# A language adapter with layer norm on one core: the order of the beginning is changed, and where the first products get their weights

## The chip, the cores and the metric

The kernel runs on one core of one Trainium2 chip. The metric is the device time of one execution in microseconds (us), the median of the runs shown.

## What is computed

For 128 samples of 128 rows and 512 columns (float32), each with the number of one of ten languages:

```python
w1 = W1[language_ids]            # 10 tables of 512 x 128
w2 = W2[language_ids]            # 10 tables of 128 x 512
h = relu(einsum('bsh,bha->bsa', x, w1) + b1[language_ids])
y = x + einsum('bsa,bah->bsh', h, w2) + b2[language_ids]
out = x + (y - mean(y)) * rsqrt(var(y) + 1e-5) * gamma[language_ids] + beta[language_ids]
```

## The kernel before

The samples are worked in 64 pairs. Ten pairs of x fit into `x_io` (SLOTS is 20), and the results are written over x in the same slots and stored from there.

**What a pair costs on each engine.** TensorE turns the two samples (`turn_x`, L488: 8 transposes of 128x128 into `ps_T`), ScalarE copies them to `x_T` (L401), TensorE makes the first product (`first_products`, L497 for b1, L504 for 8 products in float32, recorded as 16 matmuls), ScalarE takes relu and rounds it (`high_h`, L415), VectorE takes the rest of the rounding (`low_h`, L631). The second product (`second_product`, L525) is three matmuls of 512 columns for each sample, high by high, high by low and low by high, added into a bank of `ps_y` that VectorE (L644) or ScalarE (L431, every fourth sample; b2 is then added by a matmul, L519) has seeded with x + b2. ScalarE squares (L421), VectorE scales by gamma, inverts the deviation and finishes (L663, L668, L676). GpSimd adds beta to x (L358) and forms the mean (L353).

**TensorE's loop.** Iteration p does the second product of pair p - 2, turns pair p + 1, and does the first product of pair p (L552 to L573).

**The tables.** gamma, beta and b2 of all ten languages are needed on all 128 partitions. b2 is loaded there by a broadcast of 2.6 MB (L282). gamma and beta are loaded as 30 rows, cut into three bf16 parts (gamma on VectorE, L590 to L596; beta, and then b2 with its mean taken off by ScalarE, on GpSimd, L336 to L341), and spread over the partitions by 20 matmuls against a one-hot table (L544, "spread"). Six PSUM banks take the result in turn, and ScalarE (L457) or VectorE (L684) copies it out. For the first four samples b2 is put into the bank by such a matmul as well (`put_b2`, L511), before VectorE adds x (`seed_early`, L654). W2 is loaded into the x slots of pairs 5 to 9 in five chunks of two languages, its row means are taken off, and it is split into `w2_high` (ScalarE, L407) and `w2_low` (VectorE, L625). W1 is loaded into `w1_all` in five chunks (L287) in runs of 512 bytes. The first six pairs (STAGE_HBM) take their two W1 tables from HBM, also in runs of 512 bytes; later ones take one by a DMA from `w1_all` and the other by a copy of ScalarE (L440).

**What sets the order.** Every engine's order is written out by hand, with semaphores. The queue of SyncE (SP) issues nearly all transfers, in this order (L252 to L305): ids, gamma rows, x of pair 0, W1 of pair 0, W2 chunks 0 and 1, x 1, W1 of pair 1, W2 chunks 2 to 4, x 2, W1 of pair 2, b2, x 3, W1 of pair 3, all five chunks of W1, then, after waits for gamma and beta, x 4, W1 of pairs 4 and 5, and x 5 to 9, each behind the split of a chunk of W2. From then on, for each pair p: W1 of pair p + 6, the store of pair p, the load of pair p + 9. TensorE's beginning is: turn pair 0, 20 spread matmuls, turn pair 1, first product 0, turn pair 2, first product 1, and then the loop proper, whose first second product waits for all of W2:

```python
if p >= FIRST:
    n = p - FIRST
    if n == 0:
        pe.wait_ge(w2_low_ready, L)
    for b in range(2):
        second_product(2 * n + b, langs[n][b])
pe.wait_ge(x_T_ready, p + 1)
```

ScalarE's beginning is: copy x 0, ten copies of gamma, high parts of W2 chunks 0 and 1, six copies of beta, copy x 1, and then W2 chunks 2 to 4 between copies of x and relu steps (L459 to L472).

Of the kernel before, what the change touches and what calls it, by code (L numbers as in the profile page):

```python
# [5 lines left out]
F32 = mybir.dt.float32  # L6
F32R = mybir.dt.float32r
# [6 lines left out]
SLOTS = 20  # L14
Y_BANKS = 4
# [3 lines left out]
STAGE_HBM = 6  # L19
FIRST = 2  # L20
EARLY = 2
W2_AHEAD = 2


def build(nc, x, ids, w1, b1, w2, b2, gamma, beta, out):
# [8 lines left out]
    ROWS_PAIR = X_FIRST - 1  # L34
# [3 lines left out]
    w1_rows = w1.rearrange("l (c p) a -> p l c a", c=C)  # L38
    out_pairs = out.rearrange("(n b) s h -> s n b h", b=2)
# [3 lines left out]
    SPREAD_BANKS = Y_BANKS + 2  # L43
    by_act = [n for n in range(2 * L) if n not in (L, L + 2, L + 4, L + 6)]
    by_dve = [n for n in range(2 * L) if n not in by_act]
    assert FIRST + 1 <= H_PAIRS

    with ExitStack() as ctx:
# [22 lines left out]
        cut = sb("cut", [128, 2, H], BF16)  # L71
        parts = sb("parts", [128, 3 * H], BF16)
        b2_rows = sb("b2_rows", [3 * L, H], F32)
        b2_cut = sb("b2_cut", [3 * L, 2, H], BF16)
        b1_rows = sb("b1_rows", [3 * L, A], F32)
# [8 lines left out]
        pick = sb("pick", [128, L, 128], BF16)  # L84
# [11 lines left out]
        squares = cut  # L96
# [35 lines left out]
        b2_centred = sem("b2_centred")  # L132
        seeded_act = sem("seeded_act")
# [14 lines left out]
        b2_in_bank = sem("b2_in_bank")  # L148
# [33 lines left out]

        def scalar_seeds(t):
            return len([u for u in range(t + 1) if by_scalar(u)])
# [4 lines left out]
        def scalar_copies(q):  # L189

            return q >= STAGE_HBM

        def w1_copies(q):
            return len([r for r in range(q + 1) if scalar_copies(r)])

        def w1_stagings(q):

            return sum(16 if scalar_copies(r) else 32 for r in range(q % STAGE_PAIRS, q + 1, STAGE_PAIRS))
# [35 lines left out]
        spread_banks = ps_y + ps_h  # L234
        assert len(spread_banks) == SPREAD_BANKS

        def spread_bank(n):
            return spread_banks[n % SPREAD_BANKS][:, :]

# [8 lines left out]
        def _(sp):  # L248
            def load_x(p):
# [3 lines left out]
            sp.dma_start(x_io[0:3 * L, 2 * ROWS_PAIR, :],  # L253
                         gamma.unsqueeze(0).broadcast_to([3, L, H])).then_inc(s_gamma_rows, 16)
            load_x(0)
# [4 lines left out]
            def stage_w1(q):  # L260

                langs = langs_of(sp, q)
                if q >= STAGE_PAIRS:
                    sp.wait_ge(h_summed, q - STAGE_PAIRS + 1)
                if q >= STAGE_HBM:
                    sp.wait_ge(s_w1, 16 * W_CHUNKS)
                table = w1_rows if q < STAGE_HBM else w1_all
                for b in range(1 if scalar_copies(q) else 2):
                    sp.dma_start(w1_stage[:, 2 * (q % STAGE_PAIRS) + b, :, :], table[:, bass.ds(langs[b], 1), :, :])\  # L269
                        .then_inc(w1_staged[q % STAGE_PAIRS], 16)  # L270

            sp.wait_ge(ids_ready, 1)
# [10 lines left out]
            load_x(3)  # L283
            stage_w1(3)
            for n in range(W_CHUNKS):
                langs = slice(n * LC, (n + 1) * LC)
                sp.dma_start(w1_all[:, langs, :, :], w1_rows[:, langs, :, :]).then_inc(s_w1, 16)  # L287
            sp.wait_ge(gamma_parts_ready, 1)
            sp.wait_ge(beta_parts_ready, 1)
            for p in range(4, X_FIRST):  # L290
                load_x(p)
            for q in range(STAGE_PAIRS, STAGE_AHEAD):
                stage_w1(q)
            for n in range(W_CHUNKS):
                sp.wait_ge(w2_low_ready, (n + 1) * LC)
                load_x(X_FIRST + n)

            for p in range(PAIRS - 1):
                if p + STAGE_AHEAD < PAIRS:
                    stage_w1(p + STAGE_AHEAD)  # L300
                sp.wait_ge(out_ready, 2 * p + 2)
                sp.dma_start(out_pairs[:, p, :, :], x_pair_slots(p)).then_inc(stored[p % X_PAIRS], 16)
                if p >= 1 and p - 1 + X_PAIRS < PAIRS:
                    sp.wait_ge(stored[(p - 1) % X_PAIRS], x_loads(p - 1))
                    load_x(p - 1 + X_PAIRS)  # L305
# [8 lines left out]
        def _(pool):  # L314
# [29 lines left out]
            pool.wait_ge(parts_zero, 3)  # L344
            pool.wait_ge(s_beta_rows, 16)
            cut_in_three(x_io[0:3 * L, 2 * ROWS_PAIR + 1, :], b2_cut[:, 0, :], parts[0:3 * L, H:2 * H], 0, beta_parts_ready)
            pool.wait_ge(b2_centred, 1)
            cut_in_three(b2_rows[:, :], b2_cut[:, 1, :], parts[0:3 * L, 2 * H:3 * H], 4, b2_parts_ready)
# [14 lines left out]
            pool.wait_ge(spread_dve, len(by_dve))  # L363
            for n in range(PAIRS):
# [12 lines left out]
        def _(act):  # L377
            act.wait_ge(set_ready, 4)
            nc.scalar.activation(table_load[:, :], eps[:, :], ACT.Sqrt, bias=eps[:, 0:1])
            act.dma_start(b1_rows[:, :],  # L380
                          b1.unsqueeze(0).broadcast_to([3, L, A])).then_inc(s_b1_rows, 16)
            act.dma_start(x_io[0:3 * L, 2 * ROWS_PAIR + 1, :],
                          beta.unsqueeze(0).broadcast_to([3, L, H])).then_inc(s_beta_rows, 16)
            act.dma_start(b2_rows[:, :],
                          b2.unsqueeze(0).broadcast_to([3, L, H])).then_inc(s_b2_rows, 16)
            act.wait_ge(pick_step, 3)
            nc.scalar.copy(pick[:, :, :], pick_row[:, :].unsqueeze(2).broadcast_to([128, L, 128])).then_inc(pick_ready, 1)

            act.wait_ge(s_b2_rows, 16)
            nc.scalar.activation(b2_cut[:, 1, :], b2_rows[:, :], ACT.Identity, accum_out=b2_sum[:, :])\  # L390
                .then_inc(b2_summed, 1)
            act.wait_ge(b2_summed, 1)
            nc.scalar.mul(b2_neg_mean[:, :], b2_sum[:, :], -1.0 / H).then_inc(b2_mean_ready, 1)
            act.wait_ge(b2_mean_ready, 1)
            nc.scalar.activation(b2_rows[:, :], b2_rows[:, :], ACT.Identity, bias=b2_neg_mean[:, :]).then_inc(b2_centred, 1)
# [47 lines left out]
            def step(p):  # L443
# [6 lines left out]
                q = p + STAGE_PAIRS - 1  # L450
                if q < PAIRS and scalar_copies(q):
                    copy_w1(q)
# [6 lines left out]
            copy_x(0)  # L459
# [4 lines left out]
            for n in by_act[L:]:  # L464
                copy_spread(n)
            copy_x(1)
            high_w2(2)
            high_h(0)
            high_w2(3)
            copy_x(2)  # L470
            high_h(1)
            high_w2(4)  # L472
# [10 lines left out]
        def _(pe):  # L483
            def turn_x(t):
                if t % 2 == 0:
                    pe.wait_ge(x_loaded[t // 2 % X_PAIRS], x_loads(t // 2))
                for c in range(C):
                    last = nc.tensor.transpose(ps_T[:, t % 2, c, :], x_io[:, t % SLOTS, c * 128:(c + 1) * 128],  # L488
                                               identity[:, :])
                last.then_inc(x_turned, 1)  # L490

            def first_products(p):
# [7 lines left out]
                if scalar_copies(p):  # L500
                    pe.wait_ge(w1_copied, w1_copies(p))
# [8 lines left out]
            def put_b2(t, lang):  # L510
                nc.tensor.matmul(ps_y[t % Y_BANKS][:, :], of_lang(pick, lang), parts[:, 2 * H:3 * H],  # L511
                                 start=True, stop=True).then_inc(b2_in_bank, 1)

            def second_product(t, lang):
# [3 lines left out]
                if by_scalar(t):  # L518
                    nc.tensor.matmul(bank, is_lang[:, t:t + 1].broadcast_to([128, S]), parts[:, 2 * H:3 * H],  # L519
# [9 lines left out]
            pe.wait_ge(identity_ready, 1)  # L529
            turn_x(0)  # L530
            turn_x(1)
            pe.wait_ge(pick_ready, 1)
            pe.wait_ge(parts_zero, 3)
            pe.wait_ge(gamma_parts_ready, 1)
            for n in range(2 * L):
                if n == L:
                    pe.wait_ge(beta_parts_ready, 1)
                gone = n - SPREAD_BANKS
                if gone in by_act:
                    pe.wait_ge(spread_act, by_act.index(gone) + 1)  # L540
                if gone in by_dve:
                    pe.wait_ge(spread_dve, by_dve.index(gone) + 1)
                table = parts[:, 0:H] if n < L else parts[:, H:2 * H]
                nc.tensor.matmul(spread_bank(n), pick[:, n % L, :], table, start=True, stop=True).then_inc(spread, 1)  # L544

            pe.wait_ge(ids_ready, 1)
            langs = {0: langs_of(pe, 0)}
            pe.wait_ge(b1_parts_ready, 1)
            pe.wait_ge(is_lang_ready, 1)
            pe.wait_ge(spread_act, len(by_act))  # L550
            pe.wait_ge(spread_dve, len(by_dve))
            for p in range(PAIRS):  # L552
# [183 lines left out]
```

## Time and profile before

| | us |
|---|---|
| median of 3 runs (316.99 to 318.69) | 318.01 |
| the profiled execution | 316.75 |
| its span | 315.0 |
| TensorE busy | 289.5 (92%) |
| VectorE busy | 289.8 (92%) |
| ScalarE busy | 263.0 (83%) |
| GpSimd busy | 186.2 (59%) |

The profile is of one execution, and its span is 1.75 us under that execution's time. Busy time of TensorE is a record of pipelined matmuls whose ends are modelled, so the interval between starts says more than their durations. The profile moved 94.03 MB, at 298 GB/s over the span.

### The profile page before, as it was taken

The page shows a single profiled execution, that of the slowest core. Times are in us where ns is not written, and L with a number is a line of the kernel's source. Part 1 is how long each engine was busy: PE and PEld are TensorE (multiplying, and loading weights), DVE is VectorE, ACT ScalarE, POOL GpSimd, SP SyncE. Part 2 cuts the span into 40 slices and gives each one's busy share as a digit, 9 for nine tenths or more (in the row PEclk, how much of TensorE's full clock was granted, in tenths as well). Part 3 has the DMA queues.
Part 4 walks back from the last instruction along what each step waited for, and adds up shares of the span by engine and source line. Part 5 has one row for each costly group of instructions (what it writes and reads, how often), then busy time and mean ns, then how long its engine had stood idle before and what let it go on. Part 6 is the DMA issues. An engine that isn't in the chain of part 4 may idle for free.

```text
span 315.0 us, 7506 instructions
## 1 busy us (share of the span) xinstructions
PE 289.5 (92%) x2008; PEld 253.8 (81%) x2039; DVE 289.8 (92%) x621; ACT 263.0 (83%) x601; POOL 186.2 (59%) x217
## 2 busy tenths in 40 slices
PE   1757959999999999999999999999999999999972
PEld 1237758889998888998888998888999888999861
DVE  5998856999999999999999999999999999999996
ACT  3977438889988889899989988999989988988872
POOL 2960742666655666565566665656656566665562
PEclk9968779999999999999999999999999999999998
DMA  5999999899999999899898989999898889885324
GB/s 155 332 389 372 293 331 390 276 340 352 358 347 328 321 313 302 302 318 318 292 315 313 299 309 310 318 302 311 290 319 311 315 304 311 286 291 202 116 110 177
DMA packets 56441, 94.03 MB, mean 298 GB/s; under 512 B 3387, under 2 KB 14711, under 8 KB 56273
## 3 DMA queue, kind: packets, MB, share of 16 engines
q1 hardware_dynamic: 56302, 93.41, 87.4%
q8 instruction: 18, 0.29, 0.4%
q14 instruction: 22, 0.18, 0.2%
q10 hardware_dynamic: 99, 0.14, 0.1%
HBM read 44.78 MB, written 33.55 MB: 249 GB/s over the span
## 4 chain that ended last, share of the span: by engine, by line
PE 79%; SPq 10%; issue 3%; DMA 3%; DVE 2%; DVEq 1%; ACT 0%
PE ps_h L504 33%; PE ps_y L525 28%; PE ps_T L488 16%; SPq L287 5%; DMA x_io<-in_x 2%; PE ps_h L497 2%; SPq L269 2%; SPq L257 1%; SPq L282 1%; DVE ps_y L663 1%; DVE ps_y L644 1%; SPq L172 1%; SPq L250 1%; DVEq L172 1%; DMA ids_raw<-in_itok_B 1%
## 5 line engine op out<-in xcount | busy, mean ns | idle before, releaser
L358 POOL TENSOR_TENSOR x_io<-x_io,beta_all 128x512 f32<-128x512 f32 x128 | 163.0, 1284 | 37.3 <-DVE ps_y L644 27.9
L504 PE MATMUL ps_h<-x_T,w_stage 128*128 128x128 f32 x1024 | 126.2, 277 | 0.0
L504 PEld LDWEIGHTS ps_h<-x_T,w_stage 128*128 128x128 f32 x1024 | 121.0, 194 | 0.8
L421 ACT ACTIVATE cut<-ps_y,row_sum 128x512 bf16<-128x512 f32 x128 | 87.9, 687 | 16.3 <-PE ps_y L525 11.4
L676 DVE SCALAR_TENSOR_TENSOR x_io<-ps_y,rstd,x_io 128x512 f32<-128x512 f32 x128 | 90.2, 747 | 2.6 <-DVE rstd L668 0.3
L663 DVE SCALAR_TENSOR_TENSOR ps_y<-ps_y,neg_mean,gamma_all 128x512 f32<-128x512 f32 x128 | 90.3, 750 | 1.7 <-ACT cut L421 1.7
L488 PE MATMUL ps_T<-identity,x_io 128*128 128x128 f32 x512 | 69.4, 280 | 11.2 <-DMA x_io<-in_x 10.1
L488 PEld LDWEIGHTS ps_T<-identity,x_io 128*128 128x128 f32 x512 | 62.2, 145 | 20.8 <-issue 12.6
L401 ACT COPY x_T<-ps_T 128x1024 f32<-128x1024 f32 x64 | 63.5, 992 | 6.7 <-PE ps_T L488 6.5
L525 PE MATMUL ps_y<-w_high,h_high 128*128 x128 | 62.3, 486 | 3.9 <-DVE w_low L625 2.2
L644 DVE SCALAR_TENSOR_TENSOR ps_y<-x_io,b_all 128x512 f32<-128x512 f32 x93 | 62.9, 704 | 0.0
L353 POOL TENSOR_TENSOR neg_mean<-row_sum,neg_over_h 128x2 f32<-128x2 f32 x64 | 12.9, 201 | 79.0 <-DVE ps_y L644 50.5
L525 PE MATMUL ps_y<-w_high,h_low 128*128 x128 | 51.2, 400 | 0.0
L525 PE MATMUL ps_y<-w_low,h_high 128*128 x128 | 50.6, 395 | 0.0
L440 ACT COPY w_stage<-w_all 128x512 f32 x58 | 36.0, 621 | 10.3 <-issue 8.7
L631 DVE SCALAR_TENSOR_TENSOR h_low<-ps_h,h_high 128x256 fp32r<-128x256 f32 x64 | 26.9, 420 | 4.3 <-ACT h_high L415 4.3
L525 PEld LDWEIGHTS ps_y<-w_high,h_high 128*128 128x128 f32 x128 | 24.9, 194 | 6.6 <-issue 4.9
L415 ACT ACTIVATE h_high<-ps_h 128x256 fp32r<-128x256 f32 x64 | 24.3, 380 | 5.8 <-PE ps_h L504 5.6
L525 PEld LDWEIGHTS ps_y<-w_high,h_low 128*128 128x128 f32 x128 | 24.3, 190 | 5.7
L525 PEld LDWEIGHTS ps_y<-w_low,h_high 128*128 128x128 f32 x128 | 24.7, 193 | 2.3
L421 ACT ACTIVATION_READ_ACCUMULATOR cut<-ps_y,row_sum 128x1 f32 x128 | 24.8, 194 | 0.0
L424 ACT ACTIVATE std<-sq_sum,eps 128x2 f32<-128x2 f32 x64 | 18.9, 295 | 2.1
(67 smaller groups left out, 150.9 us busy)
## 6 DMA issues: line engine op xcount, KB each, us to landing
x_io<-in_x SPq DMA_DIRECT2D x64, 512.0 KB, 5.1
out<-x_io SPq DMA_DIRECT2D x63, 512.0 KB, 3.9
w_stage<-w_all SPq DMA_DIRECT2D x58, 256.0 KB, 3.3
w_stage<-in_L_cond_W SPq DMA_DIRECT2D x12, 256.0 KB, 6.5
x_io<-in_L_cond_W SPq DMA_DIRECT2D x5, 512.0 KB, 7.8
b_all<-in_L_cond_b SPq DMA_DIRECT2D x1, 2560.0 KB, 14.3
w_all<-in_L_cond_W SPq DMA_DIRECT2D x5, 512.0 KB, 7.2
out<-x_io SPq DMA_DIRECT2D x2, 256.0 KB, 2.0
```

The source lines that it names most:

```text
L358: nc.gpsimd.tensor_tensor(x_slot(t), x_slot(t), of_lang(beta_all, lang), ALU.add).then_inc(x_beta_ready, 1)
L401: nc.scalar.copy(x_T[:, slots, :, :].rearrange("p b c s -> p (b c s)"), ps_T[:, :, :, :].rearrange("p b c s -> p (b c s)")).then_inc(x_T_r ...
L415: nc.scalar.activation(flat(h_high[:, p % H_PAIRS, :, :]), pair_of(ps_h[p % 2]), ACT.Relu)\
L421: nc.scalar.activation(squares[:, t % 2, :], ps_y[t % Y_BANKS][:, :], ACT.Square, scale=-float(H), bias=stat(row_sum, t), accum_out=stat(s ...
L440: nc.scalar.copy(w1_stage[:, 2 * (q % STAGE_PAIRS) + 1, :, :].rearrange("p c a -> p (c a)"), w1_all[:, bass.ds(lang, 1), :, :].rearrange(" ...
L488: last = nc.tensor.transpose(ps_T[:, t % 2, c, :], x_io[:, t % SLOTS, c * 128:(c + 1) * 128], identity[:, :])
L504: last = nc.tensor.matmul(bank[:, b * S:(b + 1) * S], w1_stage[:, 2 * (p % STAGE_PAIRS) + b, c, :], x_T[:, (2 * p + b) % 4, c, :], start=F ...
L525: last = nc.tensor.matmul(bank, h_part[:, h, b, :], of_lang(w2_part, lang), start=False, stop=False, skip_group_check=True)
L631: nc.vector.scalar_tensor_tensor(flat(h_low[:, p % H_PAIRS, :, :]), pair_of(ps_h[p % 2]), 0.0, flat(h_high[:, p % H_PAIRS, :, :]).bitcast( ...
L644: nc.vector.scalar_tensor_tensor(ps_y[t % Y_BANKS][:, :], x_slot(t), 1.0, of_lang(b2_all, langs[b]), ALU.mult, ALU.add, accum_out=stat(row ...
L663: nc.vector.scalar_tensor_tensor(bank, bank, stat(neg_mean, t), of_lang(gamma_all, langs[b]), ALU.add, ALU.mult).then_inc(scaled, 1)
L676: nc.vector.scalar_tensor_tensor(x_slot(t), ps_y[t % Y_BANKS][:, :], stat(rstd, t), x_slot(t), ALU.mult, ALU.add).then_inc(out_ready, 1)
```

## The change

- **Transfers.** All five chunks of W2 are issued ahead of x 0. Then come W1 and x of pairs 0 to 4 (W1 of 0 to 3), then b2, behind a wait for the cut parts of b1, b2, beta and gamma, then x 5, W1 of 4, x 6, W1 of 5. The chunks of `w1_all` move into the steady loop, one each in its first five turns. W1 of 12 pairs (before: 6) comes from HBM, both tables by DMA, in runs of 2 KB; for that, x of these pairs is turned with a step of four columns. `x_io` has 24 slots (before: 20). In the steady loop the store of pair p - 3 follows the load of pair p + 7.
- **Tables.** gamma and beta are cut in two float32r parts in place of three bf16 parts. The three small row loads of ScalarE's queue are issued before its table load, beta first, and gamma and beta have 20 rows in place of 30. The mean of b2 moves from ScalarE to VectorE. The cast table `pick` (ScalarE) becomes a 128x10 table on GpSimd, `signed_pick`.
- **Order.** TensorE spreads gamma first, then turns pair 0, spreads five rows of beta, does the first half of pair 0, spreads the other five, and does the first half of pair 1. VectorE takes the means of all W2 chunks before any low part. ScalarE makes the high parts of three chunks right after gamma. GpSimd's beta adds wait until all of W2 is split. b2 of the first four samples is added by a matmul in the second product.

```diff
-SLOTS = 20
+SLOTS = 24
-STAGE_HBM = 6
+STAGE_HBM = 12
+STORE_LAG = 3
+W2_AHEAD = 3
+SPREAD_HALF = 5
...
+    w1_runs = w1.rearrange("l (p c) a -> p l c a", c=C)
...
-    SPREAD_BANKS = Y_BANKS + 2
-    by_act = [n for n in range(2 * L) if n not in (L, L + 2, L + 4, L + 6)]
+    SPREAD_BANKS = 5
+    BETA_BANKS = 3
+    by_dve = [L + 3, L + 5, L + 6]
...
+            for n in range(W_CHUNKS):
+                load_w2(n)
+            load_x(0)
             sp.wait_ge(ids_ready, 1)
             stage_w1(0)
-            load_w2(0)
-            load_w2(1)
             load_x(1)
             stage_w1(1)
-            for n in range(2, W_CHUNKS):
-                load_w2(n)
             load_x(2)
+            load_x(3)
             stage_w1(2)
+            load_x(4)
+            stage_w1(3)
+            sp.wait_ge(b1_parts_ready, 1)
+            sp.wait_ge(b2_parts_ready, 1)
+            sp.wait_ge(beta_parts_ready, 1)
+            sp.wait_ge(gamma_parts_ready, 1)
             sp.dma_start(b2_all[:, :, :], b2.partition_broadcast(128)).then_inc(s_b2, 16)
+            load_x(5)
+            stage_w1(4)
+            load_x(6)
+            stage_w1(5)
+
+            for p in range(PAIRS - 1 + STORE_LAG):
                 if p + STAGE_AHEAD < PAIRS:
                     stage_w1(p + STAGE_AHEAD)
+                ahead = p + X_FIRST
+                if ahead < X_PAIRS:
+                    load_x_behind_w2(ahead)
+                elif ahead < PAIRS:
+                    sp.wait_ge(stored[ahead % X_PAIRS], x_loads(ahead - X_PAIRS))
+                    load_x(ahead)
+                if p < W_CHUNKS:
+                    load_w1(p)
+                if p >= STORE_LAG:
+                    store(p - STORE_LAG)
...
+            pool.wait_ge(w2_low_ready, L)
             for n in range(PAIRS):
                 langs = langs_of(pool, n)
...
             for n in range(L):
                 copy_spread(n)
             for n in range(W2_AHEAD):
                 high_w2(n)
+            copy_x(0)
+            for n in by_act:
+                if L <= n < L + SPREAD_HALF:
+                    copy_spread(n)
+            high_w2(3)
             copy_x(1)
             high_h(0)
+            high_w2(4)
+            for n in by_act:
+                if n >= L + SPREAD_HALF:
+                    copy_spread(n)
             copy_x(2)
             high_h(1)
...
+                rows_of = "s (p c) -> s c p" if t // 2 < STAGE_HBM else "s (c p) -> s c p"
+                columns = x_slot(t).rearrange(rows_of, c=C)
                 for c in range(C):
+                    last = nc.tensor.transpose(ps_T[:, t % 2, c, :], columns[:, c, :], identity[:, :])
...
+            for n in range(L):
+                spread_rows(n)
+            pe.wait_ge(identity_ready, 1)
+            turn_x(0)
+            turn_x(1)
+            pe.wait_ge(beta_parts_ready, 1)
+            for n in range(L, L + SPREAD_HALF):
+                spread_rows(n)
+            pe.wait_ge(b1_parts_ready, 1)
+            pe.wait_ge(is_lang_ready, 1)
+            first_half(0)
+            for n in range(L + SPREAD_HALF, 2 * L):
+                spread_rows(n)
+            pe.wait_ge(spread_act, len(by_act))
+            pe.wait_ge(spread_dve, len(by_dve))
+            first_half(1)
+            pe.wait_ge(ids_ready, 1)
+            langs = {p: langs_of(pe, p) for p in range(FIRST)}
+            pe.wait_ge(b2_parts_ready, 1)
+            pe.wait_ge(w2_low_ready, L)
...
+            mean_of_w2(0)
+            centre_b2()
+            for n in range(1, W_CHUNKS):
+                mean_of_w2(n)
+            low_w2(0)
+            low_w2(1)
+            low_w2(2)
+            copy_spread(by_dve[0])
+            dve.wait_ge(spread_act, L)
+            seed_x(0)
+            low_w2(3)
             low_h(0)
+            for n in by_dve[1:]:
+                copy_spread(n)
+            dve.wait_ge(spread, 2 * L)
             low_w2(4)
+            dve.wait_ge(spread_act, len(by_act))
+            seed_x(1)
+            low_h(1)
```

## Rows read from the trace of the kernel before

**Rows 1.** Windows of the whole span: busy time by engine, TensorE's clock, DMA share, GB/s

```profile
core 0: us, PE busy (x) PEld busy (x) DVE busy (x) ACT busy (x) POOL busy (x), PEclk, DMA share, GB/s
0.00:53.08 53.08, 35.42 (x181) 26.41 (x183) 40.38 (x77) 33.49 (x65) 25.87 (x37) 0.87 1.00 320
53.08:293.19 240.11, 240.11 (x1738) 215.89 (x1765) 230.55 (x506) 216.95 (x505) 149.70 (x168) 1.00 0.90 308
```

**Rows 2.** Chain of waits, 0 to 56 us: start, length, what

```profile
21.61 5.96 SPq L287
...
36.40 6.59 DMA x_io<-in_x
```

**Rows 3.** TensorE's timeline, 0 to 56 us

```profile
23.40 2.94 PE L504 MATMUL ps_h<-x_T,w_stage 128*128 128x128 f32 x16
...
32.21 0.73 PE L525 MATMUL ps_y<-w_high,h_high 128*128 x1 [2.24 <-DVE w_low L625]
...
43.12 1.94 PE L488 MATMUL ps_T<-identity,x_io 128*128 128x128 f32 x8 [3.51 <-DMA x_io<-in_x]
...
49.66 1.95 PE L504 MATMUL ps_h<-x_T,w_stage 128*128 128x128 f32 x16
51.37 0.48 PE L525 MATMUL ps_y<-w_high,h_high 128*128 x1
...
53.08 1.04 PE L488 MATMUL ps_T<-identity,x_io 128*128 128x128 f32 x8
53.95 0.27 PE L497 MATMUL ps_h<-is_lang,b_parts 128*128 128x256 bf16 x1
```

**Rows 4.** ScalarE's timeline, 0 to 56 us

```profile
11.07 2.00 ACT L457 COPY gamma_all<-ps_y 128x512 f32<-128x512 f32 x4
...
15.84 2.55 ACT L407 ACTIVATE w_high<-x_io,w_neg_mean 128x512 fp32r<-128x512 f32 x4
...
23.42 1.01 ACT L401 COPY x_T<-ps_T 128x1024 f32<-128x1024 f32 x1 [2.18 <-PE ps_T L488]
```

**Rows 5.** VectorE's timeline, 0 to 56 us

```profile
5.35 0.41 DVE L590 CAST cut<-x_io 30x512 bf16<-30x512 f32 x1 [1.67 <-DMA x_io<-in_L_cond_gamma]
5.80 0.74 DVE L593 SCALAR_TENSOR_TENSOR x_io<-cut,later_part,x_io 30x512 f32<-30x512 bf16 x1
...
13.64 1.21 DVE L617 TENSOR_REDUCE w_sum<-x_io 128x2 f32<-128x1024 f32 x1
...
17.37 4.34 DVE L625 SCALAR_TENSOR_TENSOR w_low<-x_io,w_neg_mean,w_high 128x512 fp32r<-128x512 f32 x4
```

**Rows 6.** GpSimd's timeline, 0 to 56 us

```profile
14.36 1.55 POOL L336 TENSOR_SCALAR b_cut<-b_rows,later_part 30x512 bf16<-30x512 f32 x1
15.99 1.15 POOL L339 TENSOR_TENSOR b_rows<-b_rows,b_cut 30x512 f32<-30x512 f32 x1
```

**Rows 7.** Windows, as rows 1, of shorter stretches

```profile
4.00:10.00 6.00, 3.40 (x12) 2.16 (x13) 4.41 (x9) 2.63 (x5) 2.13 (x2) 1.00 0.93 281
10.00:20.00 10.00, 5.81 (x17) 1.29 (x15) 9.60 (x13) 10.00 (x20) 9.48 (x8) 0.93 1.06 366
...
30.00:40.00 10.00, 7.40 (x37) 6.12 (x37) 8.38 (x22) 5.47 (x12) 6.33 (x8) 0.83 1.18 294
...
50.00:80.00 30.00, 30.00 (x217) 26.78 (x220) 28.22 (x63) 27.06 (x64) 17.47 (x20) 1.00 0.98 337
```

**Rows 8.** Groups by line and shape, weight loads and matmuls, 53 to 297 us

```profile
L504 PEld LDWEIGHTS ps_h<-x_T,w_stage 128*128 128x128 f32 x912 | 106.3, 192 | 0.6
L488 PEld LDWEIGHTS ps_T<-identity,x_io 128*128 128x128 f32 x455 | 53.1, 140 | 7.6
...
L504 PE MATMUL ps_h<-x_T,w_stage 128*128 128x128 f32 x912 | 111.2, 275 | 0.0
L488 PE MATMUL ps_T<-identity,x_io 128*128 128x128 f32 x456 | 59.0, 272 | 0.0
```

**Rows 9.** Issues of x loads, 60 to 300 us: time to landing

```profile
DMA to landing us min/median/max: 4.2/4.9/6.2
```

More of the change, by code:

```diff
@@ L38, in build @@
     w1_rows = w1.rearrange("l (c p) a -> p l c a", c=C)
+    w1_runs = w1.rearrange("l (p c) a -> p l c a", c=C)
     out_pairs = out.rearrange("(n b) s h -> s n b h", b=2)
-    SPREAD_BANKS = Y_BANKS + 2
-    by_act = [n for n in range(2 * L) if n not in (L, L + 2, L + 4, L + 6)]
-    by_dve = [n for n in range(2 * L) if n not in by_act]
+    SPREAD_BANKS = 5
+    BETA_BANKS = 3
+    by_dve = [L + 3, L + 5, L + 6]
+    by_act = [n for n in range(2 * L) if n not in by_dve]
     assert FIRST + 1 <= H_PAIRS
@@ L67, in build @@
         b2_all = sb("b2_all", [128, L, H], F32)
[L71 to L75, printed above, removed]
+        squares = sb("squares", [128, 2, H], BF16)
+        b2_parts = sb("b2_parts", [128, H], BF16)
+        table_parts = w2_low[:, L - 2:L, :]
+        rounded = b2_all[0:2 * L, 0:2, :].bitcast(F32R)
+        gamma_rows = b2_all[0:2 * L, 2, :]
+        beta_rows = b2_all[0:2 * L, 3, :]
+        b1_rows = b2_all[0:3 * L, 4, 0:A]
+        b2_rows = b2_all[0:3 * L, 5, :]
+        b2_cut = squares[0:3 * L, 0, :]
+        b1_cut = squares[0:3 * L, 1, 0:A]
         b1_parts = sb("b1_parts", [128, A], BF16)
@@ L147, in build @@
         spread_dve = sem("spread_dve")
-        b2_in_bank = sem("b2_in_bank")
         x_turned = sem("x_turned")
@@ L187, in vector_seeds @@
             return t + 1 - scalar_seeds(t)
[L189 to L194, printed above, removed]
         def w1_stagings(q):
-            return sum(16 if scalar_copies(r) else 32 for r in range(q % STAGE_PAIRS, q + 1, STAGE_PAIRS))
+            return sum(32 if r < STAGE_HBM else 16 for r in range(q % STAGE_PAIRS, q + 1, STAGE_PAIRS))
         def wait_seed(engine, t):
@@ L266, in stage_w1, with load_w1 @@
                     sp.wait_ge(s_w1, 16 * W_CHUNKS)
-                table = w1_rows if q < STAGE_HBM else w1_all
-                for b in range(1 if scalar_copies(q) else 2):
+                table = w1_runs if q < STAGE_HBM else w1_all
+                for b in range(2 if q < STAGE_HBM else 1):
                     sp.dma_start(w1_stage[:, 2 * (q % STAGE_PAIRS) + b, :, :], table[:, bass.ds(langs[b], 1), :, :])\
                         .then_inc(w1_staged[q % STAGE_PAIRS], 16)
+            def load_w1(n):
+                langs = slice(n * LC, (n + 1) * LC)
+                sp.dma_start(w1_all[:, langs, :, :], w1_rows[:, langs, :, :]).then_inc(s_w1, 16)
@@ L288, in _ @@
[L288 to L298, printed above, removed]
+            load_x(4)
+            stage_w1(3)
+            sp.wait_ge(b1_parts_ready, 1)
@@ L377, in _ @@
         def _(act):
+            act.dma_start(beta_rows,
+                          beta.unsqueeze(0).broadcast_to([2, L, H])).then_inc(s_beta_rows, 16)
+            act.dma_start(b1_rows,
+                          b1.unsqueeze(0).broadcast_to([3, L, A])).then_inc(s_b1_rows, 16)
+            act.dma_start(b2_rows,
+                          b2.unsqueeze(0).broadcast_to([3, L, H])).then_inc(s_b2_rows, 16)
             act.wait_ge(set_ready, 4)
             nc.scalar.activation(table_load[:, :], eps[:, :], ACT.Sqrt, bias=eps[:, 0:1])
[L380 to L395, printed above, removed]
             def copy_x(p):
@@ L449, in step @@
                     copy_x(p + 1)
-                q = p + STAGE_PAIRS - 1
-                if q < PAIRS and scalar_copies(q):
-                    copy_w1(q)
+                if STAGE_HBM <= p + 1 < PAIRS:
+                    copy_w1(p + 1)
                 high_h(p)
@@ L517, in second_product @@
                 wait_seed(pe, t)
-                if by_scalar(t):
-                    nc.tensor.matmul(bank, is_lang[:, t:t + 1].broadcast_to([128, S]), parts[:, 2 * H:3 * H],
+                if without_b2(t):
+                    nc.tensor.matmul(bank, is_lang[:, t:t + 1].broadcast_to([128, S]), b2_parts[:, :],
                                      start=False, stop=False, skip_group_check=True)
@@ L527, in second_product, with first_half @@
                 last.then_inc(adapted, 1)
[L529 to L552, printed above, removed]
-                if p >= FIRST:
-                    n = p - FIRST
-                    if n == 0:
-                        pe.wait_ge(w2_low_ready, L)
-                    for b in range(2):
-                        second_product(2 * n + b, langs[n][b])
+            def first_half(p):
                 pe.wait_ge(x_T_ready, p + 1)
@@ L563, in _, with spread_rows @@
                 first_products(p)
-                if p < PAIRS - 1:
-                    langs[p + 1] = langs_of(pe, p + 1)
-                if p < EARLY:
-                    if p == 0:
-                        pe.wait_ge(b2_parts_ready, 1)
-                    for b in range(2):
-                        put_b2(2 * p + b, langs[p][b])
+            def spread_rows(n):
+                gone = spread_gone(n)
+                if gone in by_act:
+                    pe.wait_ge(spread_act, by_act.index(gone) + 1)
+                if gone in by_dve:
+                    pe.wait_ge(spread_dve, by_dve.index(gone) + 1)
+                nc.tensor.matmul(spread_bank(n), signed_pick[:, n % L:n % L + 1].broadcast_to([128, 128]),
+                                 table_parts[:, n // L, :], start=True, stop=True).then_inc(spread, 1)
+            pe.wait_ge(pick_ready, 1)
+            pe.wait_ge(parts_zero, 4)
+            pe.wait_ge(gamma_parts_ready, 1)
+            for n in range(L):
[18 more added lines that the diff above has]
+            pe.wait_ge(w2_low_ready, L)
+            for p in range(FIRST, PAIRS):
+                n = p - FIRST
+                for b in range(2):
+                    second_product(2 * n + b, langs[n][b])
+                first_half(p)
+                langs[p] = langs_of(pe, p)
             for n in range(PAIRS - FIRST, PAIRS):
@@ L585, in _ @@
             nc.vector.tensor_scalar(lang_ids[:, :], ids_fix[:, 1, :], 0.0, float(L - 1), ALU.max, ALU.min).then_inc(ids_ready, 1)
-            def cut_in_three(table, rounded, to, first, ready):
-                for k in range(2):
-                    nc.vector.tensor_copy(rounded, table).then_inc(cut_step, 1)
-                    dve.wait_ge(cut_step, first + 2 * k + 1)
-                    nc.vector.scalar_tensor_tensor(table, rounded, later_part[0:3 * L, k:k + 1], table,
-                                                   ALU.mult, ALU.subtract).then_inc(cut_step, 1)
-                    dve.wait_ge(cut_step, first + 2 * k + 2)
-                nc.vector.tensor_copy(to, table).then_inc(ready, 1)
             dve.wait_ge(pick_step, 3)
```

117 lines of the change are left out of this document (58 added, 59 removed).

## The prediction

> **What bounds the kernel now.** I read the windows first. From 53.08 us to 293.19 us TensorE has no idle time: 56 iterations in 240.11 us, 4.288 us each, at full clock, while VectorE is busy 230.55 us of it, 96% [rows 1]. That stretch is TensorE's, and nothing in the change shortens its matmuls. The change can only move the moment at which it begins. Before 53.08 us TensorE is busy 35.42 us, so 17.7 us of the beginning are idle [rows 1].
>
> The chain of waits says what holds the beginning: SP's queue, issuing the five chunks of W1 from 21.61 us (the first alone takes 5.96 us) up to 36.40 us, and then the load of x 4, 6.59 us [rows 2]. TensorE's timeline shows the same from the other side. Its first second product starts at 32.21 us, after a wait of 2.24 us for the last low part of W2. It then stands 3.51 us until x 4 lands at 43.12 us, and restarts at half speed: its 8 transposes take 1.94 us, against 1.04 us at full clock [rows 3]. At 4.288 us an iteration, a second product at 32.21 us should have led to the transposes of 53.08 us (three iterations and one second product later) at 32.21 + 12.9 + 1.7 = 46.8 us. So 6.3 us go to the stall and the slow clock behind it, and whatever time the first second product starts earlier comes on top.
>
> **The change, part by part.** I work out when the first second product starts.
>
> *W2 ahead of x.* 2.62 MB of W2, 0.52 MB of x 0 and 0.2 MB of small rows come first. DMA moved 281 GB/s from 4 to 10 us and 366 GB/s from 10 to 20 us [rows 7]. I take 366, since the first stretch was full of 512-byte runs and small rows: bytes flow from about 4.2 us, so x 0 lands at about 13.3 us (at 281 GB/s: 16 us). The last chunk of W2 lands at about 11.9 us.
>
> *gamma first.* The gamma rows landed at 5.35 us, and five steps followed. Now there are two, a cast and a combination of 0.41 and 0.74 us [rows 5]: parts ready at 6.5 us. ScalarE copies gamma at 0.50 us a row, as before [rows 4], from about 7.1 us instead of 11.07 us, until 12.1 us.
>
> *ScalarE from there.* Six high parts of W2 at 0.64 us (2.55 for four) end at 16.0 us; copying x 0, turned by 15.2 us, takes 1.01 us [rows 4], to 17.0; four copies of beta, to 19.1; two high parts, to 20.4; copy of x 1, to 21.5. Relu of pair 0 waits for TensorE until 23.3 us, then two high parts to 25.0 and the last three copies of beta to 26.6 us.
>
> *VectorE.* Mean of a chunk 1.21 us and its small step, b2's mean some 1.5 us (three short instructions on 30 rows, priced between the 0.41 and 0.74 of the cut steps): all means by 15.3 us. Six low parts at 0.70 (4.34 for four are 1.09 each, but with waits for copies between them; I take the 0.74 of a step of this form) [rows 5] end at 19.7 us. Then a beta copy, x 0 seeded (1.5), low parts 6 and 7 by 23.0, relu rest 0, two beta copies, and the last low parts by about 27.4 us.
>
> *TensorE.* Ten spreads (7 to 12 us), pair 0 turned at 13.4 to 15.2, beta spreads to 18.6, x 1 turned and the first product 0 (2.94 us with a slow start [rows 3]) to 23.3, five spreads to 26.0. It waits for the last beta copy, 26.6 us, does the first half of pair 1 (2.8 us warm, nearly twice that cold), and reads two languages. The low parts are ready by then. The first second product starts at 29.4 us at best, 32 at worst; I take 30.5 us, 1.7 us ahead of before.
>
> *From there.* The b2 matmuls of the first four samples replace the four puts of b2 in the beginning, and cost the second products about 4 x 0.23 = 0.9 us. For a clock that is not up yet I add 0.6 us. The transposes that start at 53.08 us now start at 30.5 + 14.6 + 0.9 + 0.6 = 46.6 us. **Gain 6.5 us, if transfers keep up.**
>
> *Transfers.* In front of b2 stand W2, x 0 to 4 and W1 of four pairs, 7.3 MB, landed at about 25 us; x 4 is needed only at about 36 us. SP's wait ahead of b2 ends with GpSimd's b2 parts: beta parts about 9 us, five short steps for b1, then five steps of 1.55, 1.15 and less [rows 6], about 18.5 us. SP's queue then has 6 us of transfers ahead, so nothing runs dry; if it did, x 5, W1 of 4 and all behind would slip. b2 lands at about 31 to 32 us; VectorE needs it at about 33 us, after the first squares. Up to pair 12 the queue then has 12.1 MB by W1 of 5, and for each pair W1 (0.52), x (0.52), a chunk of `w1_all` (0.52) and from the fourth on a store. At 350 GB/s for long runs (50 to 80 us moved 337, not always full) and 294 for the 512-byte runs of `w1_all` [rows 7], x 7 lands at 39 us (needed 49), x 9 at 49 (58), x 11 at 60 (66), x 12 at 66 (70). The narrowest place has some 3.5 us. After it a pair needs 1.3 MB in 4.29 us, as now. The five chunks cost the path nothing, since TensorE has prefetched pairs to work on.
>
> *Steady loop.* x is loaded with a lead of about two pairs, 8.6 us, in place of about five; a load takes 4.9 us to land, 6.2 at most [rows 9], so 0. Six copies of W1 leave ScalarE, which isn't the bound: 0. GpSimd's beta adds wait for W2; its first mean waits for seeds at 28.9 us anyway: 0. Later stores: the burst at the end is short, 0 to 0.3 us.
>
> *The step of four columns.* No transposed operand has such a step in the trace. Its bounds come from the weight loads. A transpose loads x as weights in 140 ns and the next matmul starts every (1.04 - 0.27) / 7 = 0.11 us [rows 3, 8]. The loads of the first product take 192 ns and its matmuls still start every (1.95 - 0.275) / 15 = 0.112 us [rows 3, 8]. So a load that grows by 52 ns stays hidden behind the matmul in flight: 0. Above that, every ns shows, 8 times a pair for the ten pairs 2 to 11. If the step doubles the load's whole interval of 0.11 us it costs 0.85 us a pair, 8.5 us. A gain is excluded, as the interval is the matmul's own. I take 0, since the nearest row with a slower load costs nothing.
>
> The Trainium skill speaks against this part: Advanced Engine Details and Errata, SBUF Cachelines, says that reads run at full speed only with at least two hits on each 16-byte line, and a step of four float32 has one. It gives no figure, and no run so far shows one. By that rule without cover the sum would be the 8.5 us of the second rival below; with the cover of the row it would be the forecast.
>
> **The sum.** 316.75 - 6.5 = 310.2 us for the profiled execution. It lies 1.26 us below the median of 318.01, so against the median the forecast is 311.5 us.
>
> **The rivals.**
> *Transfers bind between pairs 6 and 13.* At 300 GB/s over 31 to 66 us, 12 MB take 40 us in place of 35, and the 3.5 us of margin are overdrawn by 1.5 us, with another 1 to 2 us for the restart at half clock; or x 0 lands at 16 us and the start slips by 2.6. For: the DMA share is already 0.90 to 1.18. Against: 366 GB/s for long runs. Gain 2.5 to 4: 314.8 us.
> *The stepped weight loads are not hidden.* Pairs 2 to 11 cost 0.85 us more each, and TensorE becomes slower than the transfers it waited for. 311.5 + 8.5 = 320.0 us, slower. It decides from a load of about 0.25 us on; half of it, 4 us, still leaves a gain of 2.5 (315.7). Against: the 192 ns loads above.
> *The beginning doesn't do what it says.* TensorE waits as long as before for the last low part or beta copy, since ScalarE does more in a row, and only the stall of x 4 goes. The start stays at 32.2 to 33 us and is cold: 313.5 us. That is still faster.
> *The short lead of x in the steady loop.* Were a load to take over 8 us beside a store, each pair would wait; 0.1 us a pair is 5 us, no gain. Against: 6.2 us at most in 52 loads.
>
> **How the numbers follow.** About 0.5% (1.6 us) is what a measurement of this kernel can tell from no change. Forecast 0.52 (309 to 313.5), transfers bind 0.12, beginning no earlier 0.08, stepped loads 0.20 in all (0.12 at full price, slower; 0.08 about half, faster or same), short lead or another slip 0.08. Faster: 0.52 + 0.12 + 0.08 minus a little, 0.70; same 0.13; slower 0.17. The range runs from 308.0 (start at 29.4 us with a warm clock, and a fast measurement) to 319.5, just short of the full price of the stepped loads, whose upper part is what I leave out.
>
> **What would show it.** Right: the first L525 matmul (its new line) at 29.5 to 32 us, no wait of TensorE for x or W1 over 0.5 us afterwards, the iteration at 4.29 us from the first on, and the gapless stretch ending some 6 us earlier. Weight loads of the transposes near 190 ns with matmuls still 0.11 us apart would confirm the cover; iterations of 5.1 us up to pair 11 and 4.29 after would show the second rival; waits for x between 60 and 75 us the first. Wrong altogether: a second product after 34 us.

## The result: 2.2% slower, 325.39 us against 318.35 us

The changed kernel takes 325.39 us (median of 4 runs, 324.93 to 325.93), the kernel before 318.35 us beside it. The ratio is 1.0224, with a 95% interval of 1.0178 to 1.0269. The forecast was 311.5 us, faster, and the range ended at 319.5 us. The stretches and reads below are those of one profiled execution of each kernel.

The beginning did nearly what was forecast. TensorE's timeline of the changed kernel around its first second product (L553 is now that line, L521 the transposes):

```profile
27.30 1.70 PE L521 MATMUL ps_T<-identity,x_io 128*128 128x128 f32 x8 [0.68 <-ACT beta_all L485]
...
31.89 0.59 PE L553 MATMUL ps_y<-w_high,h_high 128*128 x1
...
47.16 1.12 PE L521 MATMUL ps_T<-identity,x_io 128*128 128x128 f32 x8
48.12 0.27 PE L529 MATMUL ps_h<-is_lang,b_parts 128*128 128x256 bf16 x1
...
73.40 1.04 PE L521 MATMUL ps_T<-identity,x_io 128*128 128x128 f32 x8
```

The transposes of x 6 start at 47.16 us, against 53.08 us before [rows 3]: 5.9 us gained, 6.5 forecast. There is no wait for x or W1 behind them. The six iterations up to 73.40 us take 4.373 us each.

From there on the kernel loses. The windows of the changed kernel, in the columns of rows 1:

```profile
47.16:73.40 26.24, 26.24 (x190) 23.88 (x189) 24.94 (x55) 20.41 (x49) 16.17 (x18) 1.00 1.07 367
73.40:305.00 231.60, 227.62 (x1605) 199.29 (x1604) 209.75 (x458) 197.92 (x457) 136.81 (x153) 1.00 0.91 295
```

The second stretch was all TensorE's in the kernel before: 240.11 us busy of 240.11 [rows 1]. Now TensorE shows 4 us of gaps. The loss is larger than that, since matmul records overlap and so cover part of a gap. The last transposes start at 305.54 us, 51 iterations after 73.40: (305.54 - 73.40) / 51 = 4.552 us each. Before, they started at 297.35 us, 57 iterations after 53.08: 4.285 us. The loss is 51 x 0.267 = 13.6 us. With 5.9 us gained in front and 6 x 0.088 = 0.5 us lost between, it makes 8.2 us, and the span grew from 315.0 to 323.3 us.

What became slower is in no group of busy time, since it is no engine work: the reads of the language numbers into each engine's registers (`TENSOR_LOAD`, one per pair and engine). These lines give the shortest, median and longest read in ns. PEldq, DVEq and ACTq are the instruction queues of TensorE, VectorE and ScalarE. The kernel before, 75 to 295 us:

```profile
L172 PEldq TENSOR_LOAD <-lang_ids x52: 536/1329/1809, 75.3 to 294.0; - x52
L172 DVEq TENSOR_LOAD <-lang_ids x52: 529/1354/1770, 75.7 to 294.3; - x52
L172 ACTq TENSOR_LOAD <-lang_ids x51: 492/1332/1742, 75.7 to 289.9; - x51
```

The changed kernel, first 35 to 70 us, then 75 to 295 us:

```profile
L182 PEldq TENSOR_LOAD <-lang_ids x9: 537/544/1270, 34.6 to 69.8; - x9
...
L182 PEldq TENSOR_LOAD <-lang_ids x48: 536/1952/2287, 78.4 to 292.9; - x48
L182 DVEq TENSOR_LOAD <-lang_ids x49: 533/1725/2173, 74.6 to 293.3; - x49
L182 ACTq TENSOR_LOAD <-lang_ids x49: 499/1704/2147, 74.5 to 293.2; - x49
```

TensorE's program has the read behind the first product of an iteration and ahead of the next second product, which needs the numbers. One iteration of the changed kernel, TensorE's read first, then the timeline:

```profile
L182 PEldq TENSOR_LOAD <-lang_ids x1: 1977/1977/1977, 201.4 to 201.4; - x1
```

```profile
200.46 0.50 SPq L294 DMA_DIRECT2D out<-x_io  x1
...
201.62 1.95 PE L536 MATMUL ps_h<-x_T,w_stage 128*128 128x128 f32 x16
...
203.66 0.17 DVE L691 RECIPROCAL rstd<-std 128x2 f32<-128x2 f32 x1 [0.76 <-issue]
203.66 0.19 PEld L553 LDWEIGHTS ps_y<-w_high,h_high 128*128 128x128 f32 x1 [0.29 <-issue]
203.67 0.50 PE L553 MATMUL ps_y<-w_high,h_high 128*128 x1
203.69 0.49 SPq L281 DMA_DIRECT2D w_stage<-w_all  x1
203.71 0.62 ACT L469 COPY w_stage<-w_all 128x512 f32 x1 [0.87 <-PE ps_h L536]
```

Before, a second product followed its first product after 1.70 us (203.94 to 205.64 us there); here it takes 2.05 us (201.62 to 203.67). The other engines' reads of this moment end together, ScalarE's and GpSimd's at 203.59 us and VectorE's at 203.61 us.

The same three intervals recur in every iteration of both kernels' steady loops. The read begins 0.20 us ahead of the first matmul of the first product. If the read is short, the second product starts 1.71 us behind that matmul (1.75 us at most). If it is long, the second product starts 0.27 us behind the end of the read (0.30 us at most). So the first product covers a read of 1.71 + 0.20 - 0.27 = 1.64 us, and what a read takes beyond that, TensorE waits. In the kernel before, 2 of 53 reads after 73.4 us were longer than the cover and cost 0.3 us in all. In the changed kernel 42 of 51 were, and their second products came 12.8 us late in all. That is nearly the whole loss of 13.6 us.

### The profile page after: what moved, and what is told of

It is laid out like the page before. It is cut to its first block, busy times and chain, and to the rows that moved or that the text cites. A ratio compares the mean times of both kernels' runs of the same rounds, so it can differ in the third digit from the quotient of the medians.

```text
span 323.3 us, 7526 instructions
## 1 busy us (share of the span) xinstructions
PE 297.2 (92%) x2039; PEld 258.9 (80%) x2039; DVE 286.5 (89%) x617; ACT 259.6 (80%) x591; POOL 186.4 (58%) x222
## 4 chain that ended last, share of the span: by engine, by line
PE 86%; DVE 6%; issue 3%; DMA 2%; ACT 1%; ACTq 1%; DVEq 0%
PE ps_h L536 35%; PE ps_y L553 30%; PE ps_T L521 17%; PE ps_y L547 2%; DMA b_all<-in_L_cond_b 2%; PE ps_h L529 2%; DVE w_low L650 2%; DVE w_sum L642 1%; DVE ps_y L686 1%; ACT squares L450 0%; DVEq L51 0%; ACTq L417 0%; DVE ps_y L677 0%; DVE beta_all L715 0%; ACT beta_all L485 0%
## 5 line engine op out<-in xcount | busy, mean ns | idle before, releaser
L450 ACT ACTIVATE squares<-ps_y,row_sum 128x512 bf16<-128x512 f32 x128 | 87.9, 687 | 16.8 <-PE ps_y L553 16.2
L521 PEld LDWEIGHTS ps_T<-identity,x_io 128*128 128x128 f32 x512 | 62.7, 153 | 13.1 <-issue 4.0
L521 PE MATMUL ps_T<-identity,x_io 128*128 128x128 f32 x512 | 68.6, 278 | 4.2 <-DMA x_io<-in_x 3.5
L553 PE MATMUL ps_y<-w_high,h_high 128*128 x128 | 63.1, 493 | 5.7 <-issue 2.4
L553 PE MATMUL ps_y<-w_high,h_low 128*128 x128 | 50.8, 397 | 0.0
L553 PE MATMUL ps_y<-w_low,h_high 128*128 x128 | 50.6, 395 | 0.0
L469 ACT COPY w_stage<-w_all 128x512 f32 x52 | 32.3, 621 | 21.2 <-PE ps_h L536 11.9
L553 PEld LDWEIGHTS ps_y<-w_high,h_high 128*128 128x128 f32 x128 | 24.5, 191 | 13.9 <-issue 11.1
L553 PEld LDWEIGHTS ps_y<-w_high,h_low 128*128 128x128 f32 x128 | 24.0, 188 | 5.7
L691 DVE RECIPROCAL rstd<-std 128x2 f32<-128x2 f32 x64 | 10.3, 161 | 20.3 <-issue 19.8
L553 PEld LDWEIGHTS ps_y<-w_low,h_high 128*128 128x128 f32 x128 | 24.2, 189 | 2.3
L450 ACT ACTIVATION_READ_ACCUMULATOR squares<-ps_y,row_sum 128x1 f32 x128 | 24.8, 193 | 0.0
```

The costliest lines, as they stand in the source:

```text
L450: nc.scalar.activation(squares[:, t % 2, :], ps_y[t % Y_BANKS][:, :], ACT.Square, scale=-float(H), bias=stat(row_sum, t), accum_out=stat(s ...
L469: nc.scalar.copy(w1_stage[:, 2 * (q % STAGE_PAIRS) + 1, :, :].rearrange("p c a -> p (c a)"), w1_all[:, bass.ds(lang, 1), :, :].rearrange(" ...
L521: last = nc.tensor.transpose(ps_T[:, t % 2, c, :], columns[:, c, :], identity[:, :])
L553: last = nc.tensor.matmul(bank, h_part[:, h, b, :], of_lang(w2_part, lang), start=False, stop=False, skip_group_check=True)
```

## The experiments

Two theories stood at first. Theory 1: the new order of the transfers in a turn (load of x, then store) lengthens the reads. Theory 2: ScalarE's copy of W1, two pairs later than before, does it. The four kernels of the first series share their runs of the kernel before (317.96 us).

**The old loop of transfers, in the new kernel.**

```diff
-                elif ahead < PAIRS:
-                    sp.wait_ge(stored[ahead % X_PAIRS], x_loads(ahead - X_PAIRS))
-                    load_x(ahead)
...
-                if p >= STORE_LAG:
-                    store(p - STORE_LAG)
+                store(p)
+                if p >= 1 and p - 1 + X_PAIRS < PAIRS:
+                    sp.wait_ge(stored[(p - 1) % X_PAIRS], x_loads(p - 1))
+                    load_x(p - 1 + X_PAIRS)
```

> The beginning is as changed, the steady loop of the transfers as before (store of pair p, then load of pair p + 11). Theory 1 (the order of stores and loads lengthens the reads of language numbers, 1.9 us on TensorE in place of 1.3, and so each iteration from 4.29 to 4.55 us): 325.4 - 51 x 0.26 = 312 us, reads near 1.3 us. Theory 2 (the later copy of W1 by ScalarE does it): 325 us, unchanged.

314.69 us, ratio 0.9911 (0.9871 to 0.9951). TensorE's reads have a median of 1.14 us, and iterations are back at 4.305 us from pair 12 on. The rest is close to the first rival of the prediction: the loads of x 12 and later are issued in between those of x 8 to 11 and the chunks of `w1_all`, x 11 lands late, and TensorE waits for it:

```profile
70.46 0.72 PE L519 MATMUL ps_T<-identity,x_io 128*128 128x128 f32 x4 [1.45 <-DMA x_io<-in_x]
```

**ScalarE's copy of W1 at its old place.**

```diff
-                if STAGE_HBM <= p + 1 < PAIRS:
-                    copy_w1(p + 1)
+                if STAGE_HBM <= p + 3 < PAIRS:
+                    copy_w1(p + 3)
```

> The changed kernel, but ScalarE copies W1 of pair p + 3 in step p, as before, in place of pair p + 1. Theory 2 (the late copy of W1 holds TensorE or lengthens the reads): 312 us. Theory 1 (the order of the transfers): 325 us, unchanged.

325.57 us, ratio 1.0219 (1.0164 to 1.0274), reads of 1.92 us. Theory 2 falls.

**Only the order in a turn: the store ahead of the load, with the lag of three pairs.**

```diff
                     stage_w1(p + STAGE_AHEAD)
+                if p >= STORE_LAG:
+                    store(p - STORE_LAG)
                 ahead = p + X_FIRST
...
-                if p >= STORE_LAG:
-                    store(p - STORE_LAG)
```

> The changed kernel with the store of pair p - 3 ahead of the load of pair p + 7 in each turn, so that the store reads on-chip memory earlier in the turn. Theory 1 in its narrow form (what counts is whether the store's data moves while the engines read their language numbers): iterations nearer to 4.3 us, 312 to 319 us, and other reading times. If the lag of three pairs itself costs (late loads): 325 us.

314.88 us, ratio 0.9868 (0.9819 to 0.9918). TensorE's reads have a median of 1.42 us, and iterations take 4.312 us from pair 12 on, 0.03 us more than before. So the lag costs little, and what counts is which of the two transfers is issued last in a turn. The swap also issues the store earlier against TensorE's read; this run does not separate the order from that moment.

**Both the loop and the copy as before.**

> The changed beginning with both the transfers' loop and the copy of W1 as before. Both theories: 312 us. If it stays near 325 us, neither is the cause and it lies in the 24 slots or in the tables from HBM.

316.23 us, ratio 0.99 (0.9859 to 0.9941), iterations of 4.29 us; TensorE waits 2.5 us for x 11. It agrees with the first run and adds nothing for theory 2.

The second series (the kernel before: 318.31 us) asks whether it is TensorE's read alone that costs.

**TensorE reads its numbers earlier.** Nothing in the transfers is changed.

```diff
                     turn_x(2 * p + 3)
+                if p >= FIRST:
+                    langs[p] = langs_of(pe, p)
                 first_products(p)
...
                 first_half(p)
-                langs[p] = langs_of(pe, p)
```

> The changed kernel with one thing moved: TensorE reads its language numbers between the transposes and the first product of an iteration, not behind the first product. If the slow read (1.9 us) holds TensorE only because it stands right ahead of the second product, it is now covered by matmuls in the queue: iterations of 4.3 to 4.4 us after pair 12, 313 to 318 us, with the read itself still 1.5 us or more. If the slow reads of VectorE and ScalarE bind as well, or something else than the reads does, 322 to 326 us.

311.2 us, ratio 0.9806 (0.9755 to 0.9857). The reads of this kernel, 75 to 295 us:

```profile
L182 ACTq TENSOR_LOAD <-lang_ids x52: 487/1760/2388, 74.0 to 292.7; - x52
L182 DVEq TENSOR_LOAD <-lang_ids x52: 529/1708/2299, 74.1 to 292.7; - x52
L182 PEldq TENSOR_LOAD <-lang_ids x52: 532/538/1734, 75.3 to 294.4; - x52
```

VectorE and ScalarE still read as slowly as in the changed kernel, and iterations take 4.287 us; no second product comes late. So the whole 13.6 us hung on TensorE's read. With it out of the way the time is close to the 311.5 us of the forecast, which speaks for the rest of the sum. The expectation was half right: I thought that the read would stay slow and be covered, but at its new moment it is short. It now begins 3.0 us behind the issue of the last store (median), not 1.1 us as in the changed kernel.

**W1 in runs of 512 bytes and x without the step, for the first 12 pairs.**

```diff
-                table = w1_runs if q < STAGE_HBM else w1_all
+                table = w1_rows if q < STAGE_HBM else w1_all
...
-                rows_of = "s (p c) -> s c p" if t // 2 < STAGE_HBM else "s (c p) -> s c p"
+                rows_of = "s (c p) -> s c p"
```

> The changed kernel with W1 of the first 12 pairs fetched in runs of 512 bytes and x turned without a step. The transposes' weight loads should go from 207 to 140 ns and iterations of pairs 2 to 11 from 4.37 to 4.29 us, 0.9 us in all. If the 2 KB runs were worth anything, waits for x or W1 appear between 40 and 75 us and eat it: 324.5 to 328 us; otherwise 324.5 us. The steady loop after pair 12 stays at 4.55 us in either case.

324.79 us, ratio 1.0214 (1.018 to 1.0248), no different from the changed kernel. The weight loads of the transposes, 35 to 70 us, with the step (changed kernel) and then without it:

```profile
L521 PEld LDWEIGHTS ps_T<-identity,x_io 128*128 128x128 f32 x64 | 9.0, 207 | 0.7
```

```profile
L521 PEld LDWEIGHTS ps_T<-identity,x_io 128*128 128x128 f32 x64 | 7.5, 140 | 1.1
```

The step costs 67 ns a load. The five iterations behind the transposes of x 6 take 4.352 us with it and 4.266 us without it. So 0.086 us an iteration shows, 11 ns for each of the 8 transposes, and 56 ns are covered. The 2 KB runs did move data faster, 374 GB/s against 324 GB/s from 50 to 70 us, and x 12 landed 4.2 us ahead of its transposes against 0.6 us. But no wait for x or W1 came in either kernel, so the time did not need it.

**The store last in the first six turns, first from then on.**

> The changed kernel, with the store behind the load in the first six turns, as changed, and the store ahead of the load from then on. Theory 1: the iterations of 4.55 us become 4.29, without the waits for x that the run with the old loop showed near 65 to 75 us: 311.5 to 313 us. If the store's place doesn't matter: 325 us.

313.23 us, ratio 0.9879 (0.9828 to 0.993). No waits for x; iterations of 4.314 us from pair 12 on, as with the store always first.

**The kernel before, with the order of its load and its store swapped.** The load is now that of pair p + 8, one pair less ahead.

```diff
+                if p >= 2 and p - 2 + X_PAIRS < PAIRS:
+                    sp.wait_ge(stored[(p - 2) % X_PAIRS], x_loads(p - 2))
+                    load_x(p - 2 + X_PAIRS)
                 sp.wait_ge(out_ready, 2 * p + 2)
                 sp.dma_start(out_pairs[:, p, :, :], x_pair_slots(p)).then_inc(stored[p % X_PAIRS], 16)
-                if p >= 1 and p - 1 + X_PAIRS < PAIRS:
-                    sp.wait_ge(stored[(p - 1) % X_PAIRS], x_loads(p - 1))
-                    load_x(p - 1 + X_PAIRS)
```

> The kernel before with only the order in each turn changed: the load of pair p + 8 first, then the store of pair p. Theory 1 (a store as the last transfer of a turn lies in time over the reads of the language numbers): reads near 1.9 us on TensorE, iterations near 4.5 us, 318 + 13 = 328 to 333 us. If the order costs only together with the lag of three pairs or the 24 slots: 318 us.

320.98 us, ratio 1.0107 (1.0064 to 1.015): slower beyond the interval, but by a fifth of the 13 us that I had written. The reads, 75 to 295 us:

```profile
L172 DVEq TENSOR_LOAD <-lang_ids x52: 523/1710/2123, 73.2 to 293.8; - x52
...
L172 PEldq TENSOR_LOAD <-lang_ids x51: 535/554/2269, 77.3 to 293.4; - x51
L172 ACTq TENSOR_LOAD <-lang_ids x51: 483/1697/2169, 77.7 to 293.8; - x51
```

The order lengthens the reads of VectorE and ScalarE here as well, from 1.35 to 1.7 us. TensorE's mostly escape: 6 of 52 are longer than the cover and cost 2.1 us. They begin 0.55 us behind the issue of the last store (median), against 1.07 us in the changed kernel. Theory 1 has to be put as two conditions: the store last, and TensorE's read at the wrong distance behind it.

The third series (the kernel before: 318.58 us) asks which transfer the reads wait behind. Of the first two kernels there is one execution each.

**No stores for pairs 0 to 51.** Their results are left out; x is loaded over them.

> The changed kernel without the stores of pairs 0 to 51 (their results are not written; x is loaded over them once they are done). Theory 1 (the store, last in each turn, is what the reads of language numbers wait behind): TensorE's reads fall from 1.9 us to 0.55 to 1.4 us, iterations near 4.29 us, 311 to 312 us. If the load of x or the on-chip copy of W1 in the same burst does it: reads near 1.9 us and 325 us.

311.52 us, against 325.39 with the stores. The reads, 75 to 295 us:

```profile
L182 PEldq TENSOR_LOAD <-lang_ids x51: 532/538/2013, 77.7 to 292.6; - x51
L182 DVEq TENSOR_LOAD <-lang_ids x51: 525/531/2083, 78.1 to 292.9; - x51
L182 ACTq TENSOR_LOAD <-lang_ids x51: 485/495/2060, 78.1 to 292.9; - x51
```

It also takes a third of the traffic away (194 GB/s in this stretch against 293), so alone it would not tell the store from the sheer traffic; the run with the store ahead of the load does, with the same traffic.

**The table of pairs 12 and on from HBM, not by the on-chip transfer.**

> The changed kernel, with the one W1 table that a DMA fetches for pairs 12 and on taken from HBM in place of the on-chip table (ScalarE's copy of the other stays). Rival to theory 1: the slow reads begin exactly with pair 12, where the on-chip transfer begins, so that transfer is what they wait behind: reads back to 0.55 us and 312 us. Theory 1 (the store): reads near 1.9 us, 325 us, or somewhat more for the 512-byte runs.

325.21 us, reads of 1.83 us, iterations of 4.528 us. The on-chip transfer of W1 that begins with pair 12 is not the cause.

**The early read with the unstepped x.**

> TensorE's early read together with unstepped x and W1 of 12 pairs in 512-byte runs: 0.5 us less than the early read alone (311.2) from the six iterations at 4.29 in place of 4.37 us, 310.7 us, unless the 512-byte runs bring waits for x, then 311 to 314 us.

312.39 us (308.91 to 314.57), ratio 0.9839 (0.9784 to 0.9894). It cannot be told from the early read alone; half a microsecond is below the spread.

**The early read in the kernel before.**

> The kernel before with TensorE's read of its language numbers moved between the transposes and the first product, and nothing else. Its reads (1.3 us) are hidden already, so 318 us, iterations of 4.285 us: the early read is worth something only where reads are slow. If it brought 5 us or more here, the gain of the early read in the changed kernel would not be a repair of the change but an own gain.

316.73 us, ratio 0.995 (0.9922 to 0.9977), iterations of 4.276 us: a small gain of its own, about 1.6 us. So nearly all of the 14 us in the changed kernel are a repair.

## Why the prediction was wrong

- **The start.** The first second product came at 31.89 us, inside the 29.4 to 32 us of the text, 1.4 us after the value taken. Half of that is the last beta copy: the turn behind it began at 27.30 us, not at 26.6. The other half is a clock that was lower for longer than priced. The 16 matmuls of pair 1's first product took 3.00 us, at a granted clock of 0.63 from 29 to 32 us, so mostly at the lower level (1.2 GHz). Two traces show what that costs. They run the same transfers and tables up to there, and their turns begin 0.2 us apart. At a clock of 1.00 (store last in six turns only) the turn at 27.25 us led to the second product at 30.24 us. At 0.50 (store ahead of the load) the turn at 27.45 us led to it at 32.92 us.
- **The gain in front.** 5.9 us against 6.5. The stall for x 4 is gone. Ahead of the first second product TensorE waits for beta copies, 2.79 us on VectorE and 0.68 us on ScalarE. Two errors partly cancel here: the start was 1.4 us later than taken, and from it to the transposes of x 6 it took 15.3 us in place of 16.1. That the gain comes so close is in part luck.
- **Transfers.** They kept up: no wait for x or W1. The narrowest place was x 12, as the prediction has it: landed 4.2 us ahead of its transposes, against some 3.5 forecast. The first rival did not come, but the old loop of transfers brings waits like it (1.45 and 2.5 us).
- **The stepped loads.** Forecast 0, measured 0.088 us a pair. The Trainium skill's rule (Advanced Engine Details and Errata, SBUF Cachelines) says that accesses which each touch another 16-byte line are slower, and this trace agrees: 207 against 140 ns. The load grew by 67 ns, 15 more than the 52 that the prediction took as covered; by its own rule 8 x 15 ns, 0.12 us a pair, should show, and that is about right. The second rival, at 0.85 us a pair, was wrong.
- **The step that failed** is "Steady loop ... so 0". I priced the new loop by one question, whether x lands in time, and it did: loads took 5.1 us to land (median; 7.3 at most), and from pair 16 on x stood ready 8 us or more ahead of use. I did not ask what else the moved store meets. The reads of language numbers stood in the trace of before with 1.33 us, under a cover of 1.64 us, and I never looked at them, since they count as no engine's work. With the store moved behind the load they took 1.95 us, 0.3 us more than the cover: 0.267 us an iteration, 13.6 us where the prediction has 0. The fourth rival named the loop, with a chance of 0.08, but for another mechanism (a late load), and that mechanism was not there.
- **What stays open.** Why a store delays the reads, and one that is issued last delays them more, is not shown. The traces show when. Over all kernels with stores, after 75 us, TensorE's reads have a median of 1.63 us where they begin 0.5 to 2 us behind the issue of the last store, of 0.84 us from 2 to 2.5 us, and of 0.54 us where they begin sooner than 0.5 us or over 2.5 us behind it. The two kernels with the early read moved that read alone, from 1.07 to 3.0 us and from 0.80 to 2.5 us behind the store, and it became short in both. The distance alone does not settle it: in the band from 0.5 to 2 us the median is 1.35 us in the kernel before and 1.95 us in the changed one. The same distance fits the reads up to pair 12 in the changed kernel, which stayed under the cover (0.54 to 1.27 us) though the store was already last: from 56 to 73 us they began 3.0 to 4.5 us behind the last store. No run changes the order of load and store at an equal distance.

## What to carry to other kernels

A steady loop that is bound by one engine can rest on small covers that no busy time shows: register reads, semaphores, issue. Before moving transfers in it, list what each engine's queue does between two of its big instructions, how long, and what covers it. Then try such a read at another place in the iteration, and look at its length there as well as at its cover. Here moving one line made the changed kernel 14 us faster, and the whole change a gain of 1.9% (1.4 to 2.5%).

## What the runs showed that I had not expected

- A register read of two numbers takes 0.50 to 0.54 us (median) on TensorE, VectorE, ScalarE and GpSimd when no stores are issued. On the first three it takes 1.33 to 1.35 us in the kernel before and 1.70 to 1.95 us in the changed one; on GpSimd 0.9 and 1.0 us. SP's reads stayed at 0.48 us in the changed kernel and took 1.57 us in the one before.
- A load of 128x128 float32 weights with a step of 16 bytes takes 207 ns, and 140 ns without.
- Nearly the same beginning differs by 2.7 us between executions (first second product at 30.24 to 32.92 us in the nine traces with the stepped transposes), mostly by the level at which TensorE's clock stands when the last wait of the beginning ends.
